# Attention stage of a fused transformer kernel: normalised rows turned by transposing DMAs, and a new order of the sums of squares and of the output addition

## The reference, cut to what matters

```python
h = jnp.concatenate([einsum('bhid,oi,od->bho', x, weighted_sum, weight), txt], axis=1)
xn = layernorm(h)
q, k, v = jnp.split(xn @ in_proj_weight.T + in_proj_bias, 3, axis=-1)    # 16 heads of 16
attn = l2_normalize(q) @ l2_normalize(k).T * exp(min(logit_scale, log(100)))
o = softmax(attn) @ v * head_scale
h = h + (o @ out_w.T + out_b)
h = h + ffn(layernorm(h))
```

## Time and profile before

| | |
|---|---|
| Time, median of 3 runs | 764.03 us (760.64 to 767.45) |
| The profiled execution | 763.01 us, span 761.2 us, mean granted clock 0.978 |
| PE busy | 701.7 us, 92% of the span |
| DVE busy | 662.9 us, 87% |
| ACT busy | 426.2 us, 56% |
| POOL busy | 402.9 us, 53% |
| Chain that ended last | issue 22%, DVE 22%, POOL 21%, PE 19% |

### The profile page before, as it was taken

The page is one execution under the profiler, slowest core; times in us unless marked ns, Lnnn a source line. Parts: engine busy times, 40 slices in busy tenths (PEclk is TensorE's granted clock), DMA queues, the critical chain, the costliest instruction groups (busy, mean ns, idle before and its releaser), DMA issues.

```text
span 761.2 us, 48123 instructions
## 1 busy us (share of the span) xinstructions
PE 701.7 (92%) x20167; PEld 498.4 (65%) x20167; DVE 662.9 (87%) x1591; ACT 426.2 (56%) x1098; POOL 402.9 (53%) x1094
## 2 busy tenths in 40 slices
PE   4999979988888888877999999999999999999998
PEld 3888856766777677656556666666666666666663
DVE  5789758899999999976779899988998989888986
ACT  4478745777777777853534444444444444444431
POOL 1141245566566667744446655665566656665511
PEclk9999997999999999996999999999999999999999
DMA  9987100000000000000001001100110011001100
GB/s 322 321 288 215 51 1 4 1 0 0 0 0 0 0 0 0 9 19 11 22 19 30 24 17 28 28 24 17 28 28 24 17 28 28 24 17 28 28 16 21
DMA packets 38366, 33.06 MB, mean 43 GB/s; under 512 B 24786, under 2 KB 33570, under 8 KB 38314
## 3 DMA queue, kind: packets, MB, share of 16 engines
q1 hardware_dynamic: 38314, 32.35, 14.1%
HBM read 22.64 MB, written 4.83 MB: 36 GB/s over the span
## 4 chain that ended last, share of the span: by engine, by line
issue 22%; DVE 22%; POOL 21%; PE 19%; POOLq 1%; ACT 1%; DVEq 1%; ACTq 0%
PE bank L193 4%; PE bank L195 4%; PE bank L194 4%; DVE smax L444 3%; POOL qpad L1425 3%; DVE k_t L476 3%; POOL hx L1439 2%; POOL x1b L1444 2%; DVE ss L479 2%; POOL ms L935 2%; POOL cf L925 2%; PE bank L987 2%; PE bank L976 2%; DVE qn L470 2%; DVE pr_t L462 2%
## 5 line engine op out<-in xcount | busy, mean ns | idle before, releaser
L193 PE MATMUL bank<-we_h,h_t_h 128*128 128x512 f16 x296 | 113.6, 384 | 1.1 <-DVE res L1310 0.9
L194 PE MATMUL bank<-we_l,h_t_h 128*128 128x512 f16 x296 | 112.7, 381 | 0.0
L195 PE MATMUL bank<-we_h,h_t_l 128*128 128x512 f16 x296 | 112.7, 381 | 0.0
L1310 DVE SCALAR_TENSOR_TENSOR acc<-bank,gate,acc 128x256 f32<-128x256 f32 x222 | 100.8, 454 | 4.5 <-PE bank L195 4.0
L193 PE MATMUL bank<-tokw_h,x_t_h 128*128 128x256 f16 x256 | 70.8, 277 | 11.7 <-DVE x_t_l L704 11.6
L194 PE MATMUL bank<-tokw_l,x_t_h 128*128 128x256 f16 x256 | 70.7, 276 | 0.0
L195 PE MATMUL bank<-tokw_h,x_t_l 128*128 128x256 f16 x256 | 70.7, 276 | 0.0
L288 PE MATMUL bank<-k_t,q_t 32*32 32x64 f32 x2368 | 41.7, 218 | 25.1 <-DVE k_t L476 25.0
L987 PEld LDWEIGHTS bank<-fpr_t,v 32*32 32x32 f32 x4736 | 46.6, 104 | 21.6 <-issue 21.4
L1194 ACT ACTIVATE junk<-x 128x256 f32<-128x256 f32 x37 | 15.4, 417 | 77.9 <-DVE x L1363 77.9
L288 PEld LDWEIGHTS bank<-k_t,q_t 32*32 32x32 f32 x2368 | 36.5, 107 | 33.5 <-issue 33.5
(11 more groups left out here) (233 smaller groups left out, 2198.8 us busy)
## 6 DMA issues: line engine op xcount, KB each, us to landing
xbuf<-in_x SPq DMA_DIRECT2D x32, 512.0 KB, 5.4
out<-res SPq DMA_DIRECT2D x36, 128.0 KB
we_s<-in_we SPq DMA_DIRECT2D x4, 512.0 KB, 7.3
inw<-in_in_w SPq DMA_DIRECT2D x1, 768.0 KB, 11.6
hn_t_h<-hn_r_h SPq DMA_TRANSPOSE x37, 2.3
hn_t_l<-hn_r_l SPq DMA_TRANSPOSE x37, 2.4
wrep<-in_w_rep SPq DMA_DIRECT2D x1, 512.0 KB, 4.6
h_all<-in_txt SPq DMA_DIRECT2D x1, 512.0 KB
```

The costliest lines, as they stand in the source:

```text
L193: nc.tensor.matmul(dst, a_h(c), b_h(c), start=start and c == 0, stop=False, skip_group_check=onto)
L194: nc.tensor.matmul(dst, a_h(c), b_l(c), start=False, stop=False, skip_group_check=onto)
L195: last = nc.tensor.matmul(dst, a_l(c), b_h(c), start=False, stop=stop and c == chunks - 1, skip_group_check=onto)
L1310: nc.vector.scalar_tensor_tensor(out=(res if e == E - 1 else acc)[:, :], in0=b_we[s % 2][:, k * D:(k + 1) * D], scalar=gate[p][:, e:e + 1] ...
```

## The change

TensorE no longer transposes the normalised rows, ScalarE and VectorE no longer split the turned result. ScalarE writes the rows twice, as float32 `xn` and as float16 high half, for tile i+4; GpSimd forms the low half; SyncE turns both halves by DMA into `xt` (`attn_turn`). On TensorE the V product stands in front of the query-key product. On ScalarE the bias comes first in the turn, and the squares and `kr` follow the exponential. On VectorE `on` comes before pr_t, ss before qn, and output addition and `on_t_l` (`lower`) at the end of the turn, except in the last turns.

```diff
@@ -130,15 +130,13 @@
-        xn = sb("xn", [P, D])
+        xn = [sb(f"xn{p}", [P, D]) for p in range(2)]
+        xn_r = [halves(f"xn_r{p}", [P, D]) for p in range(2)]
...
@@ -319,22 +317,16 @@
             def rows(i, p):
                 if isinstance(i, int) and i == 1:
                     pe.wait_ge(bvec_ready, 1)
+                if real(i, 1):
+                    pe.wait_ge(xn_in, 32 * (i + 2))
+                    wait(pe, a_v, i + 1)
+                    rows_times(b_v[:, 0:D], *xt[1 - p], lambda c: inw_h[:, c, 2 * D:3 * D],
+                               lambda c: inw_l[:, c, 2 * D:3 * D]).then_inc(a_vm, 1)
                 if real(i, 2):
-                    pe.wait_ge(a_xtl, i + 3)
+                    pe.wait_ge(xn_in, 32 * (i + 3))
                     pe.wait_ge(a_biased, i + 3)
                     rows_times(b_qk[p][:, :], *xt[p], lambda c: inw_h[:, c, 0:2 * D],
                                lambda c: inw_l[:, c, 0:2 * D], onto=True).then_inc(a_qkm, 1)
-                if real(i, 1):
-                    pe.wait_ge(a_xtl, i + 2)
-                    wait(pe, a_v, i + 1)
-                    rows_times(b_v[:, 0:D], *xt[1 - p], lambda c: inw_h[:, c, 2 * D:3 * D],
-                               lambda c: inw_l[:, c, 2 * D:3 * D]).then_inc(a_vm, 1)
-                if real(i, 3):
-                    pe.wait_ge(a_xn, i + 4)
-                    wait(pe, a_xtl, i + 3)
-                    for c in range(KC):
-                        last = nc.tensor.transpose(b_xt[:, c * P:(c + 1) * P], xn[:, c * P:(c + 1) * P], ident[:, :])
-                    last.then_inc(a_xnps, 1)
                 if real(i, -2):
                     pe.wait_ge(a_onl, i - 1)
                     rows_times(b_out, on_h, on_l, lambda c: outw_h[:, c, :], lambda c: outw_l[:, c, :]).then_inc(a_out, 1)
@@ -358,27 +350,50 @@
                     wait(act, a_out, i - 1)
                     nc.scalar.activation(on_h[:, :, :], b_ot[:, 0:D], ACT.Copy).then_inc(a_onh, 1)
-            def body(i, p, part=None):
-                if real(i, 2) and part != 1:
+            def rows(i, p):
+
+                if real(i, 4):
+                    settle(act, tokw_ready)
+                    wait(act, p_xnl, i + 3)
+                    wait(act, xn_in, 32 * (i + 3))
+                    at = bass.ds(i + 4, 1)
+                    for to in (xn_r[p][0], xn[p]):
+                        last = nc.scalar.activation(to[:, :], h_all[:, at, :].squeeze(1), ACT.Identity,
+                                                    bias=cf_all[:, at, NM:NM + 1].squeeze(1),
+                                                    scale=cf_all[:, at, RS:RS + 1].squeeze(1))
+                    last.then_inc(a_xn, 1)
+
+            def biased(i, p):
+
+                if real(i, 2):
                     if isinstance(i, int) and i == -2:
                         act.wait_ge(fixed_ready, 3)
                     wait(act, a_qk, i + 1)
                     nc.scalar.activation(b_qk[p][:, :], qkb_s[:, :], ACT.Copy).then_inc(a_biased, 1)
-                if real(i, 3) and part != 1:
-                    settle(act, tokw_ready)
-                    wait(act, a_xnps, i + 3)
-                    at = bass.ds(i + 3, 1)
-                    nc.scalar.activation(xn[:, :], h_all[:, at, :].squeeze(1), ACT.Identity,
-                                         bias=cf_all[:, at, NM:NM + 1].squeeze(1),
-                                         scale=cf_all[:, at, RS:RS + 1].squeeze(1)).then_inc(a_xn, 1)
+
+            def body(i, p, part=None):
                 if part == 0:
-                    return
+                    return rows(i, p)
+                if part is None or part == 2:
+                    biased(i, p)
                 if real(i, 0):
                     act.wait_ge(a_sub, i + 1)
                     wait(act, a_prt, i)
                     nc.scalar.activation(pr[:, :, :], sc[:, :, :], ACT.Exp).then_inc(a_exp, 1)
+                if real(i, 2):
+                    act.wait_ge(a_qkm, i + 3)
+                    wait(act, a_ss, i + 2)
+                    nc.scalar.activation(sq[:, :, :], b_qk[p][:, :], ACT.Square, scale=1.0 / WS).then_inc(a_sq, 1)
+                    wait(act, p_kpad, i + 1)
+                    nc.scalar.activation(kr[p][:, :], b_qk[p][:, D:2 * D], ACT.Copy, scale=ROOT * ROOT / WS).then_inc(a_qkr, 1)
                 if real(i, 0) and real(i, 1):
                     nc.scalar.activation(b_s[:, :], am_s[:, :], ACT.Copy).then_inc(a_masked, 1)
+                if part != 1:
+                    rows(i, p)
+                if real(i, 1):
+                    act.wait_ge(a_vm, i + 2)
+                    wait(act, a_av, i)
+                    nc.scalar.activation(vaug[1 - p][:, :, 0:HD], b_v[:, 0:D], ACT.Copy, scale=1.0 / WS).then_inc(a_v, 1)
                 if real(i, -3):
                     settle(act, tokw_ready)
                     act.wait_ge(a_h, i - 2)
@@ -391,24 +406,10 @@
                     act.wait_ge(a_mean, i - 2)
                     nc.scalar.activation(moment[:, :], hi, ACT.Square, bias=cf_all[:, at, MEAN:MEAN + 1].squeeze(1), scale=1.0 / SH,
                                          accum_out=cf_all[:, at, RS:RS + 1].squeeze(1)).then_inc(a_keep, 1)
-                if real(i, 2):
-                    act.wait_ge(a_qkm, i + 3)
-                    wait(act, a_ss, i + 2)
-                    nc.scalar.activation(sq[:, :, :], b_qk[p][:, :], ACT.Square, scale=1.0 / WS).then_inc(a_sq, 1)
-                    wait(act, p_kpad, i + 1)
-                    nc.scalar.activation(kr[p][:, :], b_qk[p][:, D:2 * D], ACT.Copy, scale=ROOT * ROOT / WS).then_inc(a_qkr, 1)
-                if real(i, 1):
-                    act.wait_ge(a_vm, i + 2)
-                    wait(act, a_av, i)
-                    nc.scalar.activation(vaug[1 - p][:, :, 0:HD], b_v[:, 0:D], ACT.Copy, scale=1.0 / WS).then_inc(a_v, 1)
-                if real(i, 3):
-                    act.wait_ge(a_xnps, i + 4)
-                    wait(act, a_vm, i + 2)
-                    nc.scalar.activation(xt[1 - p][0][:, :, :], b_xt[:, 0:D], ACT.Copy).then_inc(a_xth, 1)
                 if part != 2:
                     turned(i)
-            return body, turned
+            return body, turned, biased
         def attn_dve(dve):
             s3 = b_s[:, :].rearrange("p (h m) -> p h m", h=H)
@@ -422,6 +423,16 @@
                 hj = h_all[:, bass.ds(j, 1), :].squeeze(1)
                 nc.vector.scalar_tensor_tensor(out=hj, in0=b_out, scalar=1.0 / WS, in1=hj,
                                                op0=ALU.mult, op1=ALU.add).then_inc(a_h, 1)
+
+            def lower(i):
+
+                if real(i, -1):
+                    dve.wait_ge(a_onh, i)
+                if real(i, -2):
+                    added(i - 2)
+                if real(i, -1):
+                    wait(dve, a_out, i - 1)
+                    nc.vector.tensor_tensor(on_l[:, :, :], b_ot[:, 0:D], on_h[:, :, :], ALU.subtract).then_inc(a_onl, 1)
             def divisor(i):
@@ -447,23 +458,21 @@
                     wait(dve, a_exp, i)
                     nc.vector.tensor_tensor(sc[:, :, :], s3, smax[:, :].unsqueeze(2).to_broadcast([P, H, 32]),
                                             ALU.subtract).then_inc(a_sub, 1)
-                if real(i, -2):
-                    dve.wait_ge(a_onh, i - 1)
-                if real(i, -3):
-                    added(i - 3)
-                if real(i, -2):
-                    wait(dve, a_out, i - 2)
-                    nc.vector.tensor_tensor(on_l[:, :, :], b_ot[:, 0:D], on_h[:, :, :], ALU.subtract).then_inc(a_onl, 1)
+                if isinstance(i, int) and i > JOIN:
+                    lower(i - 1)
                 if early:
                     divisor(i)
+                    divided(i)
                 if real(i, 0):
                     dve.wait_ge(a_exp, i + 1)
                     nc.vector.transpose(pr_t[p][:, :, :], pr[:, :, :]).then_inc(a_prt, 1)
                 if not early and part != 2:
                     divisor(i)
-                if part != 2:
                     divided(i)
+                if real(i, 2):
+                    dve.wait_ge(a_sq, i + 3)
+                    nc.vector.tensor_reduce(ss[:, :], sq[:, :, :], AX.X, ALU.add).then_inc(a_ss, 1)
                 if real(i, 1):
                     dve.wait_ge(a_qkr, i + 2)
                     dve.wait_ge(p_rn, i + 2)
@@ -475,10 +484,6 @@
                     dve.wait_ge(p_kpad, i + 2)
                     nc.vector.transpose(k_t[:, :, :], kpad[:, :, :, :]).then_inc(a_qkt, 1)
                 if real(i, 2):
-                    dve.wait_ge(a_sq, i + 3)
-                    nc.vector.tensor_reduce(ss[:, :], sq[:, :, :], AX.X, ALU.add).then_inc(a_ss, 1)
-
-
                     dve.wait_ge(a_ss, i + 3)
                     nc.vector.scalar_tensor_tensor(out=half_ss[:, :], in0=ss[:, :], scalar=1e-24, in1=half_ls[:, :],
```

(51 more changed lines are left out.)

## The result

The changed kernel took 848.09 us in the median of its four executions (815.46 to 888.19), the kernel before 762.59 beside it. The profile is that of 815.46 us, span 813.4, and what follows accounts for it. No execution of the upper group was profiled: what is said of that group comes from its times and granted clocks alone.

What follows compares the result with a forecast made beforehand. VectorE, without idle time, was taken to bound the kernel at 6.10 us a turn. 763 us plus 29 x (1.05 for the loop + 2.0 for the clock) = 88, plus 12 for further turns, gave 863 us; range 790 to 888.

Steps and rivals of the forecast that it cites:

- the clock's term: TensorE's lowered clock after its longer waits: +2.0 us a turn over 29 turns, plus 10 us in five further turns.
- The first loop: Attention turn: k_t, scores, sums, V, product, squares, ss, qn, back to k_t; 7.15 us, 1.05 more than before.
- The idle time before ss: VectorE would idle about 1 us ahead of ss, released by sq; no idle there would be a sign of being wrong.
- The second loop: Attention turn: exponential to on_t_h on ScalarE, output addition and on_t_l on VectorE, smax, exponential; 6.8 us, hidden by the first.
- three turns in four struck, +2.0 a turn: TensorE gaps of 2.0 us mostly bring the low clock; 2.6 us per struck turn, between 0 and 3.5 a turn.
- GpSimd's subtraction "nothing": GpSimd's added 0.685 us subtraction costs nothing: 2.4 us a turn are free, and Newton's steps wait for rn anyway.
- VectorE under 75% busy: In the pure attention stage VectorE's busy share was to fall from 97% to under 75%.
- The scores' wait "about 2 us": TensorE's wait for k_t before the scores was to rise from 0.75 to about 2 us a turn.
- The rival "faster", 751 us: VectorE stays the bound at 5.7 us a turn, gaining 12 us; chance 0.04.
- Transfers, entry, join: Transposing DMAs land in 2.3 us each, costing nothing; entry 0, at most 4.6 us; feed-forward join 0, bounds -3 and +5.

Runs made afterwards that it cites:

- e1: Changed kernel with only ss put back behind k_t on VectorE; 796.84 us, ratio 1.048.
- e6: Changed kernel with only the query-key product put back in front of V on TensorE; 796.50 us, ratio 1.041.
- e2: Changed kernel with only output addition and on_t_l put back behind sc on VectorE; 816.24 us.
- e4: Changed kernel with products that nothing reads, three before the transposes of on and three before the scores, in TensorE's pauses; 806.14 us, ratio 1.058.
- e9: Changed kernel with only ScalarE's mask copy put back directly behind the exponential; 822.26, 822.47, 877.77 and 882.29 us.
- e5: e3 with GpSimd's subtraction put behind kpad, away from half_ss; 772.60 us, ratio 1.010.
- e8: e5 with ScalarE's mask copy put back directly behind the exponential; 764.83 us, ratio 1.003.
- e3: Changed kernel with the edits of e1 and e2 together; 780.09 us, ratio 1.025.
- e10: e8 with the query-key product also put back in front of V on TensorE; 767.76 us, ratio 1.007.
- e7: Changed kernel with TensorE, ScalarE and VectorE reordered for a short turn and two unread products filling TensorE's pause; 775.09 us, ratio 1.013.

## Why the prediction was right, and where it was not

- **Sign and range: right; the number by luck.** 863 forecast with 790 to 888, 848 measured. But 863 is a time that no execution had: it lies between the groups. The median of four happened to average the two, and the clock's term, 68 us, lies between the 12 of the lower group and the 80 of the upper.
- **The first loop: right.** 7.15 forecast, 7.24 measured, each step within 0.08 us. e1 and e6 open it in two ways and lose the 0.36 us down to the second loop. Its part of the time, 29 x 1.05 + 2 = 32 us, was 40: all 36 turns had it, and at 1.11 us.
- **The idle time before ss: wrong.** I looked for about 1 us and called its absence a sign of being wrong. At full clock it is 0.14 us. The loop is closed all the same (squares released by TensorE, ss right behind them, and e1 opens it); VectorE is idle earlier in the turn, 0.66 us before h_all. I had foreseen that wait, but not that it takes up most of the idle time that I put before ss.
- **The second loop: right**, 6.8 against 6.88, hidden while the first is closed (e2).
- **The clock: wrong as a rule.** The step that failed is "three turns in four struck, +2.0 a turn". In the lower group 9 to 12 turns of 36 were long, a struck turn of the steady stretch cost 1.4 to 1.5 us where I took 2.6, and the pace was 7.74 us on average where I forecast 9.2. The clock's whole part was about 12 us (e4) where 58 + 10 stood in the sum. Only in the upper group is it of that order: its four executions average 885.8 us, 80 above e4's. An estimate from the granted clocks and spans gives 215 us at the lower level in the upper group, 66 in the lower and 32 in e4, so each such microsecond goes with 0.3 to 0.5 us of time. I had read a rule from the lengths of eight pauses of a disturbed stretch and applied it to a steady loop; e9 has full clock right behind pauses of 2.03 us. I also misread a row: at 114 us the clock fell 0.25 us ahead of the sums, not in their middle. By the Trainium skill, "TensorE: Matmul & The Clock Gate", section "HAM oscillation", such a loop can be throttled again in every turn. The lower group does not show that, with 8 of 28 pauses in e9; the upper group's clocks of 0.87 to 0.885 lie nearer to it, but no trace shows its turns. What sends an execution into one or the other stays open. The changed kernel and e9 had the upper group in six executions of twelve; e1, e2, e4 and e6 had none in sixteen.
- **What I missed: the mask copy.** With the squares moved ahead of it, it releases L295 late (waits above). In the changed kernel that costs nothing (e9), since k_t is later still; with the loops open it costs 6 to 8 us (e5 to e8).
- **GpSimd's subtraction "nothing": wrong, but hidden.** Its time fitted; what it does to half_ss beside it did not. It costs 7.5 to 10 us once the loops are open (e3 to e5). I costed its own duration and not its neighbour's.
- **VectorE under 75% busy: wrong**, 82% (32.84 of 40). I took it at 9.2 us a turn; at 7.2 it is 5.9 of 7.2.
- **The scores' wait "about 2 us": right in sum**, 0.93 before L295 and 0.99 before L286.
- **The rival "faster", 751 us: wrongly priced.** It held VectorE for the only bound, 5.7 without xt_l. By the rows of e10 the loop through Newton's steps, 6.08 us, is as long as VectorE's turn was. So no placing of this change that keeps that loop has more than a little to give; the shortest turn here is e7's 6.01.
- **Transfers, entry, join: right in size.** 2.3 us to landing, and in the changed kernel no matmul waits for them. The 3.3 us before the first k_t are within the bounds, and not the transfers': in e3, e5, e8 and e10, which keep the transfers, the first k_t starts at 102.97 to 103.71, ahead of the 103.85 of the kernel before. The -3.1 behind the last k_t are at the edge of the bound of -3; their cause is not shown.

## What to carry to other kernels

Before an instruction is taken off the busiest engine, follow the longest loop of waits that crosses the engines: here it was as long (6.08 against 6.09), and in none of these orders was the relief worth anything. When an instruction is moved ahead in an engine's order, write down what now stands behind its wait (sq before the mask copy, on_t_h before smax) and close each loop with a sum from the rows; these sums held to 0.1 us, while the rule for the clock, drawn from eight pauses, did not. And cost an instruction on a free engine also by what runs beside it.

## What the runs showed of the hardware

- **A VectorE instruction held by GpSimd's.** half_ss, 128x32 with two inputs in SBUF, lasts 0.19 us in the kernel before, e5, e8 and e10. In most turns it lasts 0.32 in e1, 0.51 in the changed kernel and, varying, 0.35 to 0.70 in e3, and then it ends within about 0.05 us of the end of GpSimd's 128x256 subtraction. In e9 it lasts 0.15 in 34 of 37 turns, and the turn is still 7.15 or 7.24: in the changed kernel this time is off the loop. The Trainium skill, "GPSIMD Engine Reference", section "1. Specifications", says that GpSimd shares its SBUF interfaces with VectorE and contends with its instructions of two SBUF inputs; the traces agree, and e5 shows it by moving the subtraction.
- **Two groups of times on one core.** The same kernel took 815 to 823 us at granted clocks of 0.954 to 0.962, or 878 to 893 at 0.870 to 0.885, by nothing that was changed; with TensorE's pauses filled (e4) four executions lay within 2.1 us.
- **The same pause, different clocks.** In one trace (e9) TensorE waits 2.03 or 2.11 us before its scores 28 times, and the lower level follows 8 of them.
- **Small transposing transfers.** 128x256 halves in float16, SBUF to SBUF, land 2.3 to 3.1 us after their issue, 37 of each in the changed kernel.
